# Folding per-sample conditioning weights into low-rank factors: which operand is held in TensorE

## The reference, cut to what matters

```python
def reference(x, idA, idC, W, b, lora_A, lora_B, w_q, w_k, w_v, w_o, cond2_weight, router_w, A, Bf):
    h = x @ W.T + b + 2.0 * (x @ lora_A[idA]) @ lora_B[idA]      # first conditioning, per sample
    x = x + attention(h, w_q, w_k, w_v) @ w_o                    # 32 heads of 32, 8 key/value heads
    # second conditioning, per sample:  c = x @ cond2_weight[idC].T   (1024 x 1024 for each sample)
    c = einsum('bsi,boi->bso', x, cond2_weight[idC])
    logits = c @ router_w.T                                      # 4 experts
    gates = softmax(keep the best 2 of logits, the others -inf)
    mid = einsum('tf,erf->ter', c, A)                            # 4 experts x rank 16 = 64 columns
    x = x + einsum('te,teo->to', gates, einsum('ter,eor->teo', mid, Bf) * 4.0)
    return x
```

## Time and profile before

| | before |
|---|---|
| median of 3 runs | 1126.38 us |
| lowest, highest | 1125.52, 1132.72 us |
| the profiled execution | 1129.62 us |
| its span, first to last instruction | 1127.9 us |
| TensorE busy in the span (matmuls) | 1040.4 us, 92% |
| VectorE, ScalarE, POOL busy | 741.5, 419.7, 231.1 us |
| granted TensorE clock, mean | 0.965 |

### The profile page before, as it was taken

The page is one execution under the profiler, slowest core; times in us unless marked ns, Lnnn a source line. Parts: engine busy times, 40 slices in busy tenths (PEclk is TensorE's granted clock), DMA queues, the critical chain, the costliest instruction groups (busy, mean ns, idle before and its releaser), DMA issues.

```text
span 1127.9 us, 17356 instructions
## 1 busy us (share of the span) xinstructions
PE 1040.4 (92%) x6934; PEld 833.5 (74%) x6934; DVE 741.5 (66%) x1187; ACT 419.7 (37%) x718; POOL 231.1 (20%) x224
## 2 busy tenths in 40 slices
PE   7999997998799988999987999969889999999997
PEld 6877786876568765678665787648569898898896
DVE  6563634588887787776887968885565455455453
ACT  5212132254443444444444534552433232222311
POOL 1000020223222332223321324552311010110100
PEclk9999998999899999899998999989999999999998
DMA  6022121010411113211114113334266456546631
GB/s 245 24 71 71 66 77 28 21 44 26 130 34 35 39 35 99 51 35 34 40 45 110 44 44 109 90 116 167 74 186 216 158 164 213 187 152 203 192 126 38
DMA packets 46687, 108.23 MB, mean 96 GB/s; under 512 B 6402, under 2 KB 23938, under 8 KB 43536
## 3 DMA queue, kind: packets, MB, share of 16 engines
q1 hardware_dynamic: 36880, 72.52, 21.1%
q0 software_dynamic: 9728, 34.61, 9.9%
HBM read 77.73 MB, written 18.36 MB: 85 GB/s over the span
## 4 chain that ended last, share of the span: by engine, by line
PE 74%; DVE 18%; DMA 4%; ACT 2%; issue 1%; SPq 0%; POOL 0%; DVEq 0%; POOLq 0%; ACTq 0%
PE psP L740 16%; PE psW L1004 16%; PE psF L254 10%; PE psG L1032 7%; DVE nmax L642 4%; PE psO L806 4%; DVE q_stack L622 4%; DVE rden L655 4%; PE psP L755 4%; PE psS L782 3%; PE psT L793 3%; PE psX L1241 3%; PE psO L810 2%; PE psY L1260 2%; DVE nmax_parts L648 1%; DMA x_raw<-in_xT 1%
## 5 line engine op out<-in xcount | busy, mean ns | idle before, releaser
L740 PE MATMUL psP<-x_hl,wq 128*128 128x512 f32 x960 | 250.4, 410 | 8.6 <-DVE q_stack L622 8.6
L522 POOL TENSOR_TENSOR p_sum<-probs 128x512 f32<-128x512 f32 x128 | 164.8, 1287 | 453.2 <-ACT probs L572 453.1
L642 DVE TENSOR_REDUCE nmax<-psS 128x2 f32<-128x512 f32 x256 | 164.9, 684 | 119.2 <-PE psS L782 118.3
L740 PEld LDWEIGHTS psP<-x_hl,wq 128*128 128x128 f32 x960 | 183.9, 199 | 44.5 <-ACT u_t L528 5.6
L1004 PE MATMUL psW<-wq 128*128 128x256 f32 x1536 | 198.7, 285 | 12.1 <-DVE wq L983 9.3
L1004 PEld LDWEIGHTS psW<-wq 128*128 128x128 f32 x1536 | 192.0, 192 | 17.4 <-issue 8.2
L572 ACT ACTIVATE probs<-psT 128x512 f32<-128x512 f32 x256 | 138.9, 594 | 122.4 <-PE psT L793 122.1
L1017 DVE TENSOR_TENSOR cond_lo<-cond_raw,cond_hi 128x1024 fp32r<-128x1024 f32 x64 | 78.4, 1235 | 98.5 <-ACT cond_hi L1013 98.4
L1013 ACT ACTIVATE cond_hi<-cond_raw 128x1024 fp32r<-128x1024 f32 x64 | 66.9, 1057 | 156.4 <-PE psG L1032 147.6
L782 PEld LDWEIGHTS psS<-k_stack,q_stack 96*128 96x128 f32 x512 | 79.6, 191 | 46.3 <-DVE nmax L642 30.1
L782 PE MATMUL psS<-k_stack,q_stack 96*128 96x256 f32 x512 | 88.5, 291 | 26.3 <-DVE nmax L642 19.2
(11 more groups left out here) (123 smaller groups left out, 1267.1 us busy)
## 6 DMA issues: line engine op xcount, KB each, us to landing
cond_raw<-in_cond POOLq DMA_DIRECT2D x64, 512.0 KB, 4.2
x_raw<-in_xT SPq DMA_DIRECT2D x32, 256.0 KB, 4.2
q_stack<-q_stack SPq DMA_DIRECT2D x32, 256.0 KB, 3.0
o_scratch<-o_sb SPq DMA_DIRECT2D x64, 128.0 KB, 2.0
o_raw<-o_scratch SPq DMA_DIRECT2D x8, 1024.0 KB, 6.9
x_sb<-in_xT SPq DMA_DIRECT2D x8, 1024.0 KB, 6.6
outT<-x_sb SPq DMA_DIRECT2D x32, 256.0 KB, 2.5
q_raw<-in_Wqkv SPq DMA_DIRECT2D x24, 256.0 KB, 4.4
```

The costliest lines, as they stand in the source:

```text
L522: pool.tensor_tensor(p_sum[:, heads], probs[:, 0, heads], probs[:, 1, heads], ALU.add).then_inc(sum_done, 1)
L642: dve.tensor_reduce(nmax[:, n % 2, 2 * hp:2 * hp + 2, qt], psS[:, i % 2].rearrange("p (h k) -> p h k", h=2), AX.X, ALU.max, negate=True).t ...
L740: mm = pe.matmul(out, wq[:, i, w, k * P:(k + 1) * P], x[:, k, part], start=(k == 0 and n_ == 0), stop=False)
```

## The change

The two sides of the row's matmuls change places. A 128 x 128 block of the conditioning weight (cond_hi or cond_lo) becomes the stationary side, and the factors stream past it. The factors now lie together as ra, hi in columns 0 to 67 and lo in 68 to 135 of each block, so that cond_hi meets both in one matmul of 136 columns, and cond_lo meets hi in one of 68. A row has 8 blocks of inputs, hence 16 matmuls, of 128 x 136 and 128 x 68 alternately. The result has the inputs on the partitions: it is already turned. Eight blocks of 136 columns lie in three PSUM banks (folded: three, three and two), the two of psG and a new psG2; psX shrinks from two banks to one. The sum of the two halves of each block is made by VectorE, which writes g_t by three reductions over pairs (fold_copies). ScalarE's copy g_sb, the 8 transposes and the two copies go, and tile 7 is no longer cut. Row 0 of a batch waits for the reductions of the batch before (it waited for g_sb), that of batch 0 also for rows_done, since psG2 lies where attention had psM.

```diff
-    ra_hi, ra_lo = at("ra_hi", [P, KT, EC], F32R, R0 + 2176), at("ra_lo", [P, KT, EC], F32R, R0 + 4352)
+    ra = at("ra", [P, KT, 2 * EC], F32R, R0 + 2176)
-    psX = ctx.enter_context(nc.psum_tensor("psX", [P, 2, 512], F32))
+    psX = ctx.enter_context(nc.psum_tensor("psX", [P, 2, T], F32))
+    psG2 = ctx.enter_context(nc.psum_tensor("psG2", [P, 512], F32))
...
+    def folded(i):
+
+        out, j = (psG[:, i // 3], i % 3) if i < 6 else (psG2, i - 6)
+        return out[:, 2 * EC * j:2 * EC * (j + 1)]
+
     def cond_row(pe, n, k):
+
         r = KT * n + k
         pe.wait_ge(cond_lo_done, r + 1)
         if k == 0:
             if n == 0:
                 pe.wait_ge(ra_lo_done, 1)
                 pe.wait_ge(before.s_max, 4 * N)
+                pe.wait_ge(before.rows_done, N)
             else:
-                pe.wait_ge(g_copied, n)
-        for i, (a, w) in enumerate(((ra_hi, cond_hi[:, r % SPLIT]), (ra_hi, cond_lo[:, r % RAW]),
-                                    (ra_lo, cond_hi[:, r % SPLIT]))):
-            for half in range(2):
-                mm = pe.matmul(psG[0:EC, half], a[:, k], w[:, half * 512:(half + 1) * 512],
-                               start=(k == 0 and i == 0), stop=(k == KT - 1 and i == 2))
+                pe.wait_ge(gt_copied, 3 * n)
+        for i in range(KT):
+            cols = slice(i * P, (i + 1) * P)
+
+            pe.matmul(folded(i), cond_hi[:, r % SPLIT, cols], ra[:, k], start=(k == 0 and i % 3 == 0), stop=False,
+                      skip_group_check=True)
+            mm = pe.matmul(folded(i)[:, 0:EC], cond_lo[:, r % RAW, cols], ra[:, k, 0:EC], start=False,
+                           stop=(k == KT - 1), skip_group_check=True)
         mm.then_inc(cond_used, 1)
...
-            act.wait_ge(cond_used, KT * (n + 1))
-            nc.scalar.activation(g_sb[:], psG[0:EC].rearrange("p a b -> p (a b)"), ACT.Copy).then_inc(g_copied, 1)
...
-        def turn_copies(n):
-            for half in range(2):
-                dve.wait_ge(gt_done, 2 * n + half + 1)
-                dve.tensor_copy(g_t[:, 4 * half:4 * half + 4],
-                                psX[:, half, 0:4 * EC].rearrange("p (k e) -> p k e", k=4)).then_inc(gt_copied, 1)
+        def fold_copies(n):
+
+            dve.wait_ge(cond_used, KT * (n + 1))
+            for i, bank in enumerate((psG[:, 0], psG[:, 1], psG2)):
+                ks = slice(3 * i, min(3 * i + 3, KT))
+                parts = bank[:, 0:2 * EC * (ks.stop - ks.start)].rearrange("p (k w e) -> p k e w", w=2, e=EC)
+                dve.tensor_reduce(g_t[:, ks], parts, AX.X, ALU.add).then_inc(gt_copied, 1)
...
-        def turn_g(n):
+        def middle(n):
             if n == 0:
                 pe.wait_ge(before.o_copied, N)
-            pe.wait_ge(g_copied, n + 1)
-            for half in range(2):
-                for k in range(4):
-                    kk = 4 * half + k
-                    mm = pe.transpose(psX[:, half, k * EC:(k + 1) * EC], g_sb[:, kk * P:(kk + 1) * P],
-                                      id_sb[0:EC, 0:EC])
-                mm.then_inc(gt_done, 1)
-
-        def middle(n):
-            pe.wait_ge(gt_copied, 2 * n + 2)
+            pe.wait_ge(gt_copied, 3 * n + 3)
...
             for m in range(KT):
-                if m == 7:
-                    w_o_tile(pe, n, m, range(4))
-                    turn_g(n)
-                    w_o_tile(pe, n, m, range(4, KT))
-                elif n > 1 or m:
+                if n > 1 or m:
                     w_o_tile(pe, n, m, range(KT))
```

More of the change, by code:

```diff
@@ L383, in attend_stage @@
     st.proj_done, st.proj_act, st.proj_dve, st.s_max = proj_done, proj_act, proj_dve, s_max
+    st.rows_done = rows_done
     st.exp_done, st.pv_done, st.o_copied, st.o_stored = exp_done, pv_done, o_copied, o_stored
@@ L899, in finish_stage @@
     fb_hi_done, fb_lo_done = sem("fb_hi_done"), sem("fb_lo_done")
-    g_copied = sem("g_copied")
-    gt_done, gt_copied = sem("gt_done"), sem("gt_copied")
+    gt_copied = sem("gt_copied")
     mid_done = sem("mid_done")
@@ L1045, in ahead_scalar @@
             act.wait_ge(const_landed, 16)
-            nc.scalar.activation(ra_hi[:], ra_raw[:], ACT.Copy).then_inc(ra_hi_done, 1)
+            nc.scalar.activation(ra[:, :, 0:EC], ra_raw[:], ACT.Copy).then_inc(ra_hi_done, 1)
         for r in ROWS_SPLIT.get(s, ()):
@@ L1058, in ahead_vector @@
             dve.wait_ge(ra_hi_done, 1)
-            dve.tensor_tensor(ra_lo[:], ra_raw[:], f(ra_hi[:]), ALU.subtract).then_inc(ra_lo_done, 1)
+            dve.tensor_tensor(ra[:, :, EC:2 * EC], ra_raw[:], f(ra[:, :, 0:EC]), ALU.subtract).then_inc(ra_lo_done, 1)
         if part == 1:
@@ L1091, in gated_part @@
             act.wait_ge(gated_turned, n)
-            nc.scalar.activation(gated_hi[:], psX[:, 1, 0:T], ACT.Copy, scale=FFN_SCALE).then_inc(gated_hi_done, 1)
+            nc.scalar.activation(gated_hi[:], psX[:, 1], ACT.Copy, scale=FFN_SCALE).then_inc(gated_hi_done, 1)
         def batch(n):
@@ L1163, in gated_part @@
             dve.wait_ge(gated_hi_done, n)
[L1164 removed]
+            dve.scalar_tensor_tensor(gated_lo[:], psX[:, 1], FFN_SCALE, f(gated_hi[:]),
                                      ALU.mult, ALU.subtract).then_inc(gated_lo_done, 1)
[L1167 to L1171 removed]
+        def fold_copies(n):
[4 more added lines that the diff above has]
+                dve.tensor_reduce(g_t[:, ks], parts, AX.X, ALU.add).then_inc(gt_copied, 1)
         def add_y(n, j):
@@ L1184, in batch @@
                 if m == 7 and n:
-                    turn_copies(n)
+                    fold_copies(n)
                 if n:
@@ L1269, in first @@
             w_o_tile(pe, 1, 0, range(KT))
-            turn_g(0)
             middle(0)
```

1 line of the change is left out of this document (removed).

## The result

| | before | after |
|---|---|---|
| median | 1126.89 us (4 runs) | 1150.28 us (4 runs) |
| lowest, highest | 1125.52, 1132.72 | 1147.49, 1152.13 |
| ratio after / before | | 1.020, 95% interval 1.016 to 1.024 |
| profiled execution, its span | 1129.62, 1127.9 | 1152.13, 1150.5 |
| granted TensorE clock, mean | 0.965 | 0.961 |

Ratios leave out executions in a slower state of the chip: one of e6_triple_turns (1270.1 us, granted clock 0.768), two of e11_bf16_lo_old_head (1140.2 and 1140.4) and one of the kernel before (1141.3).

A forecast was written before the change was run, and what follows sets the result against it. TensorE was taken to bound the finishing stage, and loads each pair of a row. Batches 1 to 7 at +2.44 us (+17.1) and the head (+2.1) made +19.2 on a median of 1126.4: 1146 us, range 1137 to 1163.

The forecast's parts named there:

- The bound: Finishing stage, about 835 to 1115 us: TensorE busy in all of 40.00 us, so every nanosecond of it is time.
- The price of a row: TensorE rows: 16 load-bound pairs at 0.110 us, 1.76 us against 1.39, +0.37 a row, +2.96 a batch.
- The transposes and the cut tile: TensorE: 8 transposes go (0.49 us) and tile 7 is no longer cut (0.03), -0.52 us a batch.
- The reductions: VectorE, before the middle: 0.58, 0.58 and 0.44, together 1.6 us, hidden under tile 7 (2.87 us) by about 1 us.
- The head: Batch 0, in the tail of attention: its middle starts about 2.1 us later, bounds 1 to 5 us.
- Rival D: Rows 6 and 7 of each batch: clock falls to 1.2 GHz, +25 us, 1170 or more; chance 0.02.
- A: Rows: 128-column loads go faster, as the transposes' do; a row 1.05 us, whole 1103; chance 0.06.
- The 81 ns of the Trainium skill: Rows: load and matmul pairs at 128 columns sustain about 81 ns; a row 1.30 us, whole near 1117 us.
- B: Rows: short fp32r streams are not single pass; a row 3.52 or 2.90 us, whole 1253 or 1214; chance 0.11.
- C: Before the middle: reductions cost double, it waits 0.5 us a batch, 1.6 more in the head, 1151; chance 0.03.

The follow-up runs named there:

- e6_triple_turns: Kernel before, with each of its 8 transposes of a batch made three times: 1135.4 us, ratio 1.005 to before.
- e11_bf16_lo_old_head: Changed kernel with cond_lo in bfloat16 and batch 0 in the old form: 1130.1 us, ratio 1.000 to before.
- e1: Changed kernel, but all 16 matmuls of a row stream 136 columns: 1150.1 us, ratio 1.016 to before.
- e2: Changed kernel with the 8 matmuls on cond_lo of each row left out: 1094.2 us, ratio 0.966 to before.
- e3: Changed kernel, but each matmul on cond_lo holds only 64 of its 128 columns: 1122.6 us, ratio 0.995 to before.
- e4: Changed kernel with a row's 8 matmuls on cond_hi first, then the 8 on cond_lo: 1147.0 us, ratio 1.018 to before.
- e7_double_fold: Changed kernel with each of VectorE's three reductions made twice, one into a spare tile: 1146.1 us, ratio 1.015 to before.
- e10: Changed kernel with cond_lo in bfloat16, met by a bfloat16 copy of the factors' hi part: 1131.4 us, ratio 1.001 to before.
- e7_triple_fold: Changed kernel with each of VectorE's three reductions made three times, one behind the other: 1192.3 us, ratio 1.052 to before.
- e5_old_head: Changed kernel, but all 8 rows of batch 0 in the old form: 1146.5 us, ratio 1.012 to before.
- e9: Changed kernel, but only rows 0 to 3 of batch 0 in the old form: 1149.5 us, ratio 1.015 to before.
- e8: Changed kernel, but only rows 4 to 7 of batch 0 in the old form: 1148.6 us, ratio 1.014 to before.

## Why the prediction was right, and where it was off

**The bound.** Right: TensorE is full from the first middle to the last, and what a row costs there is time.

**The price of a row.** Right, and it is most of the result, 18.8 of 22.6 us: 16 pairs at 0.112 us against my 0.110, 1.79 us against 1.76. The extra 0.03 a row is 0.24 a batch and 1.7 over seven, which is the difference between 18.8 and 17.1. That the pair is bound by its load was argued from the slope of load durations and from the middle; e1, e2, e3 and e4 show it from four sides. The argument from the middle was weaker than it read: its loads are busy for 23.41 of 23.70 us, but so are those of the W_o tiles, whose pairs have 256 streamed columns and 0.120 us (L1004 alone, columns as in the earlier trace rows):

```profile
835.00:1110.00 275.00, 167.46 (x1308) 162.25 (x1308) 1.00 0.52 169
```

A busy load path doesn't tell the two apart; the pitch of 0.110 next to short streams did.

**The transposes and the cut tile.** -0.52 a batch: e6 gives 0.49 or 0.50 for the eight transposes (+1.00 us for 16). Right for these; the 0.03 of the cut was not tested by itself. 8 x 0.40 - 0.52 = 2.68, and the period grew by 2.69.

**The reductions.** 577, 577 and 431 ns by the profile's groups, my 0.58, 0.58 and 0.44; overlapped they take 1.42 us. Right also in that no wait stands before a middle. The cover ends about where I had it (e7_double_fold, 2.74 us of reductions), but what lies beyond may be mis-sized: I priced a failing cover at its wait, 0.5 us a batch. Behind waits of 2.0 us the price has the half clock in it; a wait of 0.5 us before these middles was not run.

**The head.** This is the step that failed. I said that rows 0 to 3 would push the chain by 1.6 us, that the split of ffn_B and the 1.6 us of reductions behind it would set the middle of batch 0, and +2.1 in all. Measured is +4.8. The push was right: the split of ffn_B ends 31.8 us after the start of row 0, where it was 30.4. But the path was another. In the timeline of the changed kernel ffn_B is split by 831.74 and row 7 ends only then; the reductions run from 832.07 to 833.49, and the tile of W_o is what the middle waits for:

```profile
830.52 1.22 DVE L1220 TENSOR_TENSOR fb_stack<-fb_raw,fb_stack 64x1024 fp32r<-64x1024 f32 x1
831.84 4.52 PE L1005 MATMUL psW<-wq 128*128 128x256 f32 x24
832.07 1.42 DVE L1181 TENSOR_REDUCE g_t<-psG 128x204 f32<-128x408 f32 x3 [0.33 <-PE psG L1042]
...
836.20 1.01 PE L1242 MATMUL psX<-g_t,x_sb 128*128 128x68 f32 x8
```

Rows 5 to 7 and most of that tile ran at 0.50. I had written of "rows 4 to 7 and the tile end before that, even with 0.37 each": at half the clock a row takes 3.4 us, so it is +2.0 and not +0.37, for three rows. Row 3, which I had at half the clock and 3.52 us, was as forecast (3.6 us, from 811.7 to 815.3).

**Rival D** had this mechanism, and I gave it 0.02, in the wrong place. For rows 6 and 7 of the batches it did not happen, as the middles had suggested. It happened in the head, where rows of short streams follow a wait of TensorE (1.64 us) and each other, without a tile between them. I had the half clock of row 3 before my eyes, and did not ask what keeps it low.

**A and B.** fp32r loads of 128 columns last 192 ns and pair at 0.112 next to short streams too: the transposes' pace is not theirs. The 81 ns of the Trainium skill (TensorE: Matmul & The Clock Gate, Back-to-back issue gap) is not met by fp32r; the bfloat16 pair of e10, 0.078, is near it. Short fp32r streams have one record and cost no more than their load, so rival B, at 0.11, is out. **C**: nothing of it was seen.

## What to carry to other kernels

Count held columns and streamed columns apart: on this chip an fp32r matmul cost here the larger of about 0.87 ns for each column held and 0.42 ns for each column streamed, plus a little, so for a pair of operands like these it is cheaper to hold the narrow one and stream the wide one: 1632 streamed columns in place of 3072 gained nothing against 16 loads in place of 6. A saved transposition is worth its 0.06 us a piece when nothing waits for it; set that against the loads that it brings. And a wait ahead of load-bound matmuls is not priced by its own length: look at the granted clock of what follows it.

## What the runs showed of the hardware that was not expected

- A busy TensorE is no sign of a full clock. In the changed kernel it is busy for 12.40 of 12.40 us at a granted 0.50, the 1.2 GHz level, in load-bound rows; the full clock comes back within the dense tile behind them, and the middle has 1.00. The same rows between dense tiles have 1.00 for 296 us. The Trainium skill (TensorE: Matmul & The Clock Gate, Why this matters for your kernels) advises to keep TensorE busy without a break to get past the low level: this stretch without a break did not.
- A wait of 2.0 us ahead of a load-bound middle cost up to 7 us (e7_triple_fold): 2.0 of wait, 3.5 in the middle and 1.5 in the tile behind it. Behind waits of 0.5 to 0.7 us middle 0 had the half clock in e6_triple_turns (7.04 us) and in e11_bf16_lo_old_head (6.23 us), but not in the kernel before (0.63) or in e5_old_head (0.70).
- What these runs don't settle is what the clock goes by. All nine kernels whose batch 0 has rows 4 to 7 in the new form (the changed one, e1 to e4, both of e7, e9, e10) have 0.50 in rows 5 to 7, and the five with the old form (before, e5, e6, e8, e11) have 1.00; streams of 136 columns in all 16 matmuls (e1_wide) didn't change it. That the middle of batch 0 has it in some kernels and not in others is left open, and with it some 5 us of an execution.
- A load of 128 bfloat16 columns lasts 96 ns, of fp32r 192; the pairs cost 0.078 (by difference) and 0.112 us.
